# Attention with exact fp32 weights: turning the weights on TensorE, or making the scores a second time with keys on partitions

## The reference, cut to what matters

```
for x (8, 512, 512), 16 heads of 32, weights (512, 512):
  q, k, v = x @ Wq.T, x @ Wk.T, x @ Wv.T, split into heads
  scores  = q @ k.T / sqrt(32);  scores[mask] = -inf
  attn    = softmax(scores) @ v  ->  out = attn @ Wo.T
  x1      = x + (out / rms(out) * rms_scale) * (1 + sc) + shift     # sc, shift from a condition vector
  result  = x1 + rotation(x1)    # quaternion products per 128 columns; the filter reduces to a gate
```

## Time and profile before

| | us |
|---|---|
| median of 3 runs (987.81 to 989.0) | 988.85 |
| span of the profiled execution | 986.2 |
| TensorE busy | 912.2 (92%) |
| VectorE busy | 707.5 (72%) |
| ScalarE busy | 638.8 (65%) |
| GpSimd busy | 523.6 (53%) |
| moved by DMA | 153.98 MB, 156 GB/s |

### The profile page before, as it was taken

How to read it: one execution, slowest core, us unless ns; L and a number is a source line. 1 busy time by engine, 2 the same in 40 slices (tenths; PEclk the granted TensorE clock), 3 DMA queues, 4 the chain that set the end, 5 groups by cost and what they waited for, 6 DMA issues and landing times.

```text
span 986.2 us, 20466 instructions
## 1 busy us (share of the span) xinstructions
PE 912.2 (92%) x6278; PEld 648.2 (66%) x6278; DVE 707.5 (72%) x1581; ACT 638.8 (65%) x1523; POOL 523.6 (53%) x441
## 2 busy tenths in 40 slices
PE   7999999999968989999999998999999999999980
PEld 5788888888845557666666665666666666666650
DVE  4522132223168888989999898899999899898878
ACT  5222222223158888888888887788888888888820
POOL 0999930000001122677666776566677666776665
PEclk9999999999979999999999999999999999999995
DMA  8855465544878547756666745666665576455111
GB/s 282 303 188 193 170 223 189 183 171 181 186 249 185 118 98 181 164 117 151 150 140 139 194 108 129 152 155 145 142 161 125 133 187 156 109 120 139 33 54 43
DMA packets 82325, 153.98 MB, mean 156 GB/s; under 512 B 8472, under 2 KB 9112, under 8 KB 82224
## 3 DMA queue, kind: packets, MB, share of 16 engines
q1 hardware_dynamic: 82224, 152.75, 57.6%
HBM read 102.35 MB, written 50.36 MB: 155 GB/s over the span
## 4 chain that ended last, share of the span: by engine, by line
PE 59%; issue 6%; DVE 5%; POOL 1%; DVEq 0%; ACT 0%; POOLq 0%
PE prob_ps L663 27%; PE out_ps L679 15%; PE score_ps L647 12%; DVE probs_T L770 2%; PE y_ps L700 2%; PE y_ps L701 1%; PE y_ps L702 1%; PE out_ps L689 1%; DVE probs L528 1%; POOL probs L1008 1%; DVE probs L754 0%; DVE probs L824 0%; DVE probs L836 0%; DVEq L520 0%; DVE probs L831 0%
## 5 line engine op out<-in xcount | busy, mean ns | idle before, releaser
L867 ACT ACTIVATE probs<-probs,least 128x512 f32<-128x512 f32 x512 | 364.3, 716 | 32.0 <-DVE inv_den L763 25.4
L663 PE MATMUL prob_ps<-ident,probs 128*128 128x128 f32 x2048 | 314.5, 281 | 26.2 <-DVE probs_T L770 25.4
L754 DVE CUSTOM_DVE_ANT_0 probs<-score_ps,mask_bias 128x512 f32<-128x512 f32 x512 | 333.1, 679 | 4.4 <-PE score_ps L647 4.4
L663 PEld LDWEIGHTS prob_ps<-ident,probs 128*128 128x128 f32 x2048 | 227.4, 141 | 159.2 <-issue 117.7
L647 PE MATMUL score_ps<-k_rows,q_rows 128*128 128x512 f32 x512 | 240.4, 477 | 12.5 <-PEq L78 9.3
L770 DVE COPY probs_T<-prob_ps 128x512 f32<-128x512 f32 x256 | 175.4, 685 | 65.0 <-PE prob_ps L663 63.1
L874 ACT ACTIVATE probs_T<-prob_ps 128x512 f32<-128x512 f32 x256 | 153.2, 598 | 76.7 <-PE prob_ps L663 72.6
L271 DVE SCALAR_TENSOR_TENSOR late<-proj,late 128x512 fp32r<-128x512 f32 x64 | 44.0, 690 | 181.3 <-ACT late L240 181.2
L679 PE MATMUL out_ps<-probs_T,v_sb 128*32 128x256 f32 x2048 | 163.0, 391 | 0.0
L528 POOL TENSOR_TENSOR late<-rot,late 128x2048 f32<-128x2048 f32 x26 | 119.1, 4580 | 66.8 <-DVE late L787 66.8
L940 POOL TENSOR_TENSOR o_T<-raw_T 128x256 f32<-128x256 f32 x64 | 47.9, 748 | 142.3 <-ACT raw_T L882 142.3
(11 more groups left out here) (112 smaller groups left out, 1349.1 us busy)
## 6 DMA issues: line engine op xcount, KB each, us to landing
q_rows<-q_scratch SPq DMA_DIRECT2D x128, 256.0 KB, 5.8
k_rows<-k_scratch SPq DMA_DIRECT2D x128, 256.0 KB, 6.7
q_scratch<-late SPq DMA_DIRECT2D x64, 256.0 KB, 2.3
k_scratch<-late SPq DMA_DIRECT2D x64, 256.0 KB, 2.3
v_scratch<-v_out SPq DMA_DIRECT2D x32, 256.0 KB, 2.0
v_sb<-v_scratch SPq DMA_DIRECT2D x8, 1024.0 KB, 10.9
raw<-in_xT SPq DMA_DIRECT2D x7, 1024.0 KB, 5.6
late<-in_x SPq DMA_DIRECT2D x28, 256.0 KB, 2.7
```

What stands on the lines that cost most here:

```text
L663: last = pe.transpose(prob_ps[:, r % 2, j * HALF + c * P:j * HALF + (c + 1) * P], probs[:, s % 2, r // 2 * 2 + c, key:key + P], ident[:, :])
L754: dve.tensor_tensor_reduce(probs[:, s % 2, r, :], score_ps[:, r % 4, :], mask_bias[:, c, :], 1.0, 3e38, ALU.add, ALU.min, least[:, s % 2, ...
L867: act.activation(probs[:, s % 2, r, :], probs[:, s % 2, r, :], ACT.Exp, bias=least[:, s % 2, r:r + 1], scale=-1.0, accum_out=den[:, s % 2, ...
```

## The change

The scores of a unit are now made twice. First with queries on partitions, as before, 23 tiles ahead, but only for the row minimum: VectorE's masked pass writes its tile back to PSUM, where nobody reads it. Each unit's 16 columns of minima are split into high and low part, turned by four transposes on TensorE, copied by VectorE to eight rows of SBUF and moved by four small DMAs into two extra rows of the unit's q rows; the k rows hold -1 there. The stacked contraction has three parts (96 rows) instead of four, plus these two rows.

The second score has keys on partitions and all 512 queries in its columns; the two extra rows subtract the minimum. ScalarE first copies the turned mask into the PSUM bank, and the matmul adds to it. There are three such banks. ScalarE takes exp out of PSUM into a ring of 12 weight tiles, which are already laid out for the value product: no turn, no copy out, no accumulator. Sums over keys are made by TensorE with a matrix of ones, four heads side by side, beside the value matmuls, which now have 512 columns. VectorE turns the sums in 32x32 blocks, inverts them, turns them back and scales the values straight out of PSUM; GpSimd's multiplication goes. Rows have three buffers instead of two, row loads six DMAs instead of eight, and the loops over batches are written out. At the end, the rotations of the last chunks of batch 6 go to GpSimd instead of VectorE. The first block gets the turned mask: one more load and one more pass of VectorE.

```diff
+TILES = TC * HG                                  # 16 tiles a unit
+RING, BANKS = 12, 3
+AHEAD, TURN_AFTER = 23, 18
+VALUE_AT, PROJECT_AT, SQUARE_AT = 2, 8, 15
+RESCALE_AT, SUMS_AT, VALUES_AT, RESIDUAL_AT = 1, 4, 5, 8
...
 Rows.load:
-        for r in range(4):
+        for r in range(3):
...
 sync, per unit u:
+                if u + 2 < U and u > 0:
+                    load_unit(u + 2)          # waits for the last score of unit u - 1
...
+            def load_least(u):
+                sp.wait_ge(row_taken, turn_place(u) + 1)
+                for i in range(HG):
+                    sp.dma_start(f32(rows.q[u % RB][3 * D:3 * D + 2, i, :]),
+                                 least_rows[2 * i:2 * i + 2, :]).then_inc(least_in[u % RB], 16)
...
 tensor:
+            def row_scores(n):
+                if row_place(n) >= 2:
+                    pe.wait_ge(row_taken, row_place(n) - 1)
+                pe.matmul(row_ps[:, row_place(n) % 2, :], rows.q[u % RB][0:3 * D, i, c * P:(c + 1) * P],
+                          rows.k[u % RB][0:3 * D, i, :], start=True, stop=True).then_inc(row_filled, 1)
...
+            def score(u, t):
+                if t == 0:
+                    pe.wait_ge(least_in[u % RB], 64 * (u // RB + 1))
+                pe.wait_ge(mask_set, TILES * u + t + 1)
+                pe.matmul(score_ps[:, (TILES * u + t) % BANKS, :], rows.k[u % RB][0:3 * D + 2, i, j * P:(j + 1) * P],
+                          rows.q[u % RB][0:3 * D + 2, i, :], start=False, stop=True,
+                          skip_group_check=True).then_inc(scored, 1)
...
+            def value(u, j):
+                pe.wait_ge(exped, TILES * u + HG * (j + 1))
+                if j == 0 and u > 0:
+                    pe.wait_ge(sums_turned, u)
+                    pe.wait_ge(o_scaled, u)
+                for i in range(HG):
+                    pe.matmul(value_ps[i * D:(i + 1) * D, :], v_sb[:, b % 2, j, h * D:(h + 1) * D],
+                              weights[:, (TILES * u + HG * j + i) % RING, :], start=(j == 0), stop=(j == TC - 1))
+                for i in range(HG):
+                    last = pe.matmul(sum_ps[i * D:(i + 1) * D, :], ones[:, :],
+                                     weights[:, (TILES * u + HG * j + i) % RING, :], start=(j == 0), stop=(j == TC - 1))
+                last.then_inc(valued, 1)
...
+            for u in range(U):
+                for t in range(TILES):
+                    n = TILES * u + t + AHEAD
+                    if n < TILES * U:
+                        row_scores(n)
+                    if n % TILES == TURN_AFTER % TILES and u + 1 < U:
+                        turn_least(u + 1)
+                    score(u, t)
+                    if t % HG == VALUE_AT and TILES * u + t >= HG + VALUE_AT:
+                        value(...)                 # the four tiles that ended three tiles ago
+                    if u >= NG and PROJECT_AT <= t < PROJECT_AT + 6:
+                        for part in (2 * (t - PROJECT_AT), 2 * (t - PROJECT_AT) + 1):
+                            project(u - NG, part)
...
 vector:
+                dve.tensor_tensor_reduce(bank, bank, mask_bias[:, c, :], 1.0, 3e38, ALU.add, ALU.min,
+                                         least[:, u % 2, c, i:i + 1]).then_inc(row_taken, 1)
...
+            def turn_sums(u):
+                dve.wait_ge(valued, TC * (u + 1))
+                dve.transpose(sums_T[:, :, :].rearrange("p n d -> p (n d)"), sum_ps[:, :]).then_inc(sums_turned, 1)
+                dve.wait_ge(sums_turned, u + 1)
+                dve.reciprocal(inv[:, :], sums_T[:, :, 0]).then_inc(inverted, 1)
+            def scale_values(u):
+                dve.wait_ge(inverted, u + 1)
+                dve.transpose(inv_T[:, :].rearrange("p (n d) -> p n d", d=D),
+                              inv[:, :].unsqueeze(2).to_broadcast([P, S // D, D])).then_inc(inv_turned, 1)
+                dve.wait_ge(inv_turned, u + 1)
+                dve.tensor_tensor(o_T[:, u % 2], value_ps[:, :], inv_T[:, :], ALU.mult).then_inc(o_scaled, 1)
+            # per tile t: row_least(n), split_least at n % 16 == 15, take_rows at n % 16 == 2,
+            # rescale at t 1, turn_sums(u - 1) at t 4, scale_values(u - 1) at t 5, residual at t 8
...
 scalar:
+            def set_mask(n):
+                if n >= BANKS:
+                    act.wait_ge(exped, n - BANKS + 1)
+                act.activation(score_ps[:, n % BANKS, :], maskT_bias[:, n % TILES // HG, :], ACT.Copy).then_inc(mask_set, 1)
+            def exp(n):
+                act.wait_ge(scored, n + 1)
+                if n >= RING:
+                    act.wait_ge(valued, (n - RING) // HG + 1)
+                act.activation(weights[:, n % RING, :], score_ps[:, n % BANKS, :], ACT.Exp, scale=-1.0).then_inc(exped, 1)
+            # per tile: exp(n), set_mask(n + 2); square at t 15
```

More of the change, by code:

```diff
@@ L194, in batch @@
                         sp.wait_ge(qk_stored[g], 64)
-                        rows.load(sp, g, g)
+                        rows.load(sp, g)
                 if more:
@@ L427, in _, with attention @@
             last.then_inc(rot_ready, 1)
-def attention(nc, x, scr, rows, late, qk_stored, mod_scr, out, mask_bias, rot, ident, wo_hi, wo_lo):
+def attention(nc, x, scr, rows, late, qk_stored, mod_scr, out, mask_bias, maskT_bias, rot, ident, wo_hi, wo_lo):
     with ExitStack() as ctx:
@@ L635, in _ @@
         def _(pe):
-            def score(b, s, r):
-                n, g, half = STEPS * b + s, s // 2, s % 2
-                p, i = g % 2, r // 2
-                if r == 0 and half == 0:
-                    seen = 32 * (NG * b + g - p) + 64
-                    pe.wait_ge(rows.q_in[p], seen)
-                    pe.wait_ge(rows.k_in[p], seen)
-                if not (known(n, 1) and r < 4):
-                    pe.wait_ge(masked, TILES * n + r - 3)
-                c = 2 * half + r % 2
-                pe.matmul(score_ps[:, r % 4, :], rows.q[:, p, i, c * P:(c + 1) * P], rows.k[:, p, i, :],
-                          start=True, stop=True).then_inc(scores, 1)
@@ L699, in project @@
                 t = slice(c * P, (c + 1) * P)
-                pe.matmul(y[:, :], o_hi[:, p, k, t], wo_hi[:, k, :], start=(k == 0), stop=False)
-                pe.matmul(y[:, :], o_hi[:, p, k, t], wo_lo[:, k, :], start=False, stop=False)
-                last = pe.matmul(y[:, :], o_lo[:, p, k, t], wo_hi[:, k, :], start=False, stop=(k == KC - 1))
-                if k == KC - 1:
+                left = o_lo if way == 2 else o_hi
+                right = wo_lo if way == 1 else wo_hi
+                last = pe.matmul(y_ps[:, :] if to is None else to, left[:, b % 2, k, t], right[:, k, :], start=(part == 0), stop=(part == 11))
@@ L726, in _ @@
-            for r in range(TILES + SCORE_AHEAD):
-                score(0, r // TILES, r % TILES)
-            batch(0, 0, first=True)
-            batch(1, 1)
-            with pe.Fori(2, B - 3, 2) as b:
-                batch(b, 0)
-                batch(b + 1, 1)
-            batch(B - 2, 0)
-            batch(B - 1, 1, last=True)
-            for k in (2, 3):
-                project(B - 2, 0, TC - 1, k, y_ps)
-            for j in range(TC):
-                value(B - 1, STEPS - 1, 1, j)
-            turn_scale(STEPS * B - 1)
@@ L807, in _ @@
-            for r in range(TILES + MASK_AHEAD):
-                mask(0, r // TILES, r % TILES)
-            batch(0, 0, first=True)
-            batch(1, 1)
-            with dve.Fori(2, B - 3, 2) as b:
-                batch(b, 0)
-                batch(b + 1, 1)
-            batch(B - 2, 0)
-            batch(B - 1, 1, last=True)
-            rescale(B - 2, 0, TC - 1)
+            dve.memset(ones[:, :], 1.0).then_inc(consts_set, 1)
+            dve.memset(least_parts[:, :, :], 0.0).then_inc(consts_set, 1)
```

593 lines of the change are left out of this document (252 added, 341 removed).

## The result

The changed kernel takes 1125.93 us (median of 3 runs, 1125.09 to 1126.63) against 988.85. The ratio is 1.139, with a 95% interval of 1.137 to 1.141: slower, inside the range of 990 to 1155, 28 us above the forecast of 1098. The profiled execution has a span of 1123.0.

The account below looks back on a forecast made before the run. TensorE's own sequence bounds the kernel before; after the change TensorE and ScalarE lock. First score at 297.9, units 751, end 16.6, tail 29.6: span 1095.6, plus 2.7 for the medians, 1098 us; range 990 to 1155.

Parts of the forecast that it names:

- First score: Before the attention units: row passes, turned minima and four DMAs take 17.2 us from block start, so 297.9 us.
- The burst: Value and sum matmuls behind every fourth score on TensorE: 2.0 us each, 2.54 from score to score over it.
- The lock: Three score banks, each preset by ScalarE, make TensorE and ScalarE wait in turn: 5.10 us per four slots, TensorE working 3.8.
- Rival 1: TensorE keeps running in the units, its own sum of 18.8 us a unit counts: 937 us; chance 0.16.
- ScalarE: In the units, exp taken at 0.50 us and mask copy at 0.49; 16.4 a unit, so ScalarE alone does not bound.
- The hand-off: Value bank between units: VectorE is done at 7.0 us, TensorE wants it at 5.5, so it waits 1.5 in slot 6.
- Rival 2: The lock holds but the value bank's hand-off hides, 31 x 1.5 us less: 1051 us; chance 0.14.
- Rival 3: The minima's DMAs land late for score 0 of a unit, slipping some 1.5 us a unit: 1145 us; chance 0.12.
- Units: Attention units: 23.8 us with projections, 22.5 without (units 1 to 3), 19.4 for unit 0.
- The sum: All units of the attention block together: 751 us, within a span of 1095.6.
- the clock: TensorE's granted clock stays full in the block, waits being 1.5 us at most; a fall to 1.2 GHz would move all upward.
- TensorE busy near 79%: Sign in the attention block that the forecast is right; above 95% would show TensorE running on instead.

Follow-up runs that it names:

- Experiment 4: The changed kernel with 23 extra matmuls into the unused projection bank, one behind each row score ahead of the first unit: 1119.86 us.
- experiment 2: The changed kernel with the burst cut in two, value matmuls one slot behind the sums, VectorE turning sums without waiting for values: 1042.47 us.
- experiment 3: The changed kernel with the burst cut in two and the value matmuls two slots behind the sums: 1028.11 us.
- experiment 1: The changed kernel with VectorE's turning of the sums and scaling of the values one slot earlier: 1109.84 us.
- experiment 7: experiment 3 plus Experiment 4's extra matmuls, with VectorE adding weight tiles in pairs so TensorE makes two groups of sums a unit instead of four: 1280.85 us.
- experiment 11: experiment 7 with GpSimd's three rotation instructions cut to 1/32 of their columns and less: 1102.27 us.
- Experiment 5: The changed kernel without ScalarE's mask copies into PSUM, the mask left out of the weights: 1097.96 us.
- experiment 9: experiment 3 plus Experiment 4's extra matmuls, with row scores behind the first 23 tiles cut to 32 of 512 columns: 990.53 us.
- experiment 10: experiment 3 plus Experiment 4's extra matmuls, with the matmuls of ones cut to 32 of 512 columns in all units but the first: 1006.38 us.
- experiment 12: experiment 3 plus Experiment 4's extra matmuls, with projection pairs spread behind slots 3, 5, ... 13, where no sums or values stand: 1004.83 us.

## Why the prediction was right, and by how much it was short

The change lost as forecast and by the mechanism that was forecast; what was short is told below, term by term.

**Block start.** Forecast 280.7, the first row score started at 281.0: right. **First score.** Forecast 297.9, measured 302.1, 4.2 late. Row passes come two in 1.64 us instead of 1.22, because TensorE's two row banks are refilled at 1.2 GHz (stage 281 to 302, PEclk 0.50). I had the row scores hidden behind VectorE; at half speed they are not. Experiment 4 supports it: at 0.90 the first score came at 299.8, 2.3 earlier.

**The burst.** Four groups of two passes, forecast 1.9 between the score's follower and the next row score, measured 1.85; 0.33 into it and 0.34 out, as from the earlier trace rows. Score to score 2.54 forecast, 2.52 measured. **The lock.** Burst to burst was to be 5.10; 711.34 to 717.28 is 5.94, of which the square (0.57) was counted apart and the entry into the burst at the lower clock (0.59 instead of 0.33) makes the rest. In a unit at full clock the whole walk can be laid beside the trace. Its bursts start at 449.39, 456.13, 461.34, 467.56 and 473.35. The stretch with the hand-off took 6.74 (forecast 6.60), the next 5.21 (5.10), the one with the turning of the minima 6.22 (6.41), the one with the square 5.79 (5.67). The plain stretch is 5.19 to 5.21 in units without projections too, where TensorE has some 3.9 us of work in it. Experiments 2 and 3 move the matmuls and the wait of VectorE that follows from it, leave nothing out, and win 83 and 98 us; with an even spread of the projections and the warm start it is 121 of the 137 us. So it is mainly the order, not the amount of work, that makes the change lose. That three banks are too few was argued from the walk: no run had a fourth. Rival 1, TensorE keeps running, is refuted for the change as it is. Its sum was nearly right for a kernel with adjacent groups (19.0 by measured distances, 18.8 forecast); the order that lets TensorE run splits them and costs 1.3.

**ScalarE.** An exp out of PSUM is 0.60 long and followed after 0.47 to 0.50, a mask copy into PSUM 0.60 and after 0.52: 0.50 and 0.49 were taken. The end at 0.62 did not come, nor the 0.52 for an exp that the prediction set beside its 0.50. ScalarE waited 1.23 for the score behind the burst where some 1.1 was forecast.

**The hand-off.** Forecast a wait of 1.5, measured 1.48 in the timeline above, and 25.0 us in 17 waits from 500 to 900. VectorE's 32x32 transposes took 0.71, where a copy's 0.6 was taken with 0.3 and 1.2 as ends:

```profile
L715 DVE STREAM_TRANSPOSE sums_T<-sum_ps 128x512 f32<-128x512 f32 x17 | 12.1, 712 | 0.0
...
L721 DVE STREAM_TRANSPOSE inv_T<-inv 128x512 f32<-128x512 f32 x17 | 12.0, 706 | 0.0
```

Rival 2, hidden hand-off, is refuted, and experiment 1 shows that the wait is on the path. Rival 3, late minima, too: score 0 of the first unit waited 0.52 for its DMA and no steady unit did. In experiments 7 and 11 there were such waits, 3.9 and 4.9 us from 500 to 900.

**Units.** With projections 23.8 forecast, 23.97 measured in 18 of the 27 such units. Units 1 to 3 were 22.5 forecast and 24.98, 23.98, 24.07 measured; unit 0 19.4 and 21.06. Eight of the later ones were 24.8 to 25.6. In units 1 to 3 one stretch each, behind the hand-off, took 7.40, 6.39 and 6.48 at 1.2 GHz instead of 5.20; unit 2 of experiment 4, at full clock, took 22.81.

**The sum.** From first to last score the forecast had 751, the trace has 773.3. The 22 us are: unit 0 1.7, units 1 to 3 5.5, the eight long units 10.7, and 27 times 0.16 less what the last one gave back. With 4.2 at the start, 1 at the tail (1075.4 to 1123.0, 47.6 against 46.6) and 0.2 between span and median (2.9 against 2.7), that is the 28 us.

**Slips in the sums.** The wait for a freed bank is 0.50 + 0.60 + 0.05 = 1.15 and not 1.14, and the five terms of the way over a burst add up to 2.56 and not 2.54. The terms named for the end of the loop (a last burst of 2.0, 2.4, 2.1 and 9.1) are 15.6, where 16.6 was taken. The 19.4 of unit 0 and the 1.9 less of the last unit have no working. None of these moves the forecast by more than 3 us.

**The step that was mis-sized** is the clock. The prediction took it as full within the block because its waits are 1.5 at most, and named its fall only as something that would move all upward. It fell in 12 short stretches between 331 and 1065, three of them in units 1 to 3, eight in the eight long units. Each cost 0.9 to 1.6 us, and the first, which was longer, 2.2; together some 15 of the 28. The Trainium skill ("TensorE: Matmul & The Clock Gate", A second HAM failure mode: psum-queue depth-cycling) tells of a kernel in which short idle times between groups of matmuls, from cycling through PSUM banks, made the clock swing between its two levels. The trace agrees in that both stand together here: before the burst of 717.28 TensorE was busy 2.93 of 4.00 us, waiting for ScalarE and VectorE in small pieces, and the burst took 3.32 instead of 1.85. That the one causes the other no run tests. Weighing that page would have put the forecast higher; it gives no price for it.

**A wrong mark.** "TensorE busy near 79%" did not show: it was 87% in the block. Busy time is made of lengths, and a matmul's length (0.40) exceeds its distance to the next (0.23), so each short idle time is partly covered, and at 1.2 GHz idle-looking slack turns into busy time. Distances between starts were the right measure; the sum of lengths was not.

**What stays open.** What of the 83 us of experiment 2 is lock and what hand-off was not separated by a run: in it both went. An estimate from the traces: the hand-off's wait (25.0 / 17, in 31 units) is some 45, the stretches at 1.2 GHz in the units some 15, and the four additional changes into and out of a group take 1.3 a unit, 41, back; some 64 are then left for the waits for mask copies, the lock. Experiment 5 leaves a doubt on its size: without the copies the time fell by 28 where the lock wanted 70, and what made up the difference there is read from the trace, not from a run. Why exactly 8 units of 27 lost their clock, in four pairs, five to eight units apart, no run tells.

## What to carry to other kernels

Work that is in order on one engine needs slack on the others for as long as its longest uninterrupted stretch: ask how many tiles the next engine holds when a burst starts, and place two short bursts rather than one long one before counting matmuls. A freed microsecond counts only after the next two waits were walked through too; experiments 5, 9 and 10 each lost about half or more of it to a wait or a clock that was not there before. And compare totals in the order that runs, not the order that counts best. By the order that runs, TensorE's sum is 20.3 us a unit, not 18.8, so next to nothing is left of the 1.6 that the change was to win on TensorE. Against the kernel before, experiment 12 has its first score 18.3 us later (300.7 against 282.4), takes 8.4 longer from the first score to the last, and ends 9.4 sooner behind it: 17 us in all.

## What the runs showed of the hardware

- The granted clock fell to 1.2 GHz in kernels whose TensorE waited 0.7 to 2.2 us at a time: from 320 us to the last score 44 us in the changed kernel, 102 in experiment 5, 280 in experiment 7. In experiments 2, 3 and 12, with waits of 0.2, 0.5 and 0.7 at most, it did not fall there at all; in the kernel before, with waits up to 1.1 and one of 3.2, for 3 us. Extra matmuls whose results nobody uses, ahead of the units, won 6 us. That the waits cause the fall was not tested by itself.
- VectorE's fp32 addition of two SBUF tiles of 128x512 took 0.69 alone and 2.90 beside GpSimd's rotation, while its passes with a source in PSUM kept 0.69. Each of the 147 slow additions ended 0.54 to 0.55 after the GpSimd instruction that it met.
- Four fp32 matmuls of 512 columns side by side in the array's column groups, in two passes, take 0.99 alone and 0.88 when another such group follows; with 32 columns 0.20.
- A fp32r matmul of 32 columns still costs 0.03 to 0.14 to the next, and of 512 columns 0.234.
